# Linear attention: the transposes of a pair's keys ahead of the next pair's query features

## What is computed

```python
def _phi(x, proj):
    return jax.nn.elu(x @ proj) + 1.0
h = _ln(x, g1, beta1)
q = _phi((h @ wq).reshape(b, s, H, DH), proj)
k = _phi((h @ wk).reshape(b, s, H, DH), proj)
v = (h @ wv).reshape(b, s, H, DH)
# per token t, with running sums over the tokens up to it:
kv = kv + k_t[..., :, None] * v_t[..., None, :]
ksum = ksum + k_t
out = einsum('bhd,bhde->bhe', q_t, kv) / (einsum('bhd,bhd->bh', q_t, ksum) + 1e-06)
```

## Time and profile before

| | us |
|---|---|
| median of three runs | 2431.95 |
| the profiled execution | 2432.54 |
| its span, first to last instruction | 2430.7 |
| linear attention in the timeline | about 1287 to 1862 |

### The profile page before, as it was taken

The page is one execution under the profiler, slowest core; times in us unless marked ns, Lnnn a source line. Parts: engine busy times, 40 slices in busy tenths (PEclk is TensorE's granted clock), DMA queues, the critical chain, the costliest instruction groups (busy, mean ns, idle before and its releaser), DMA issues. The chain is left out here.

```text
span 2430.7 us, 40493 instructions
## 1 busy us (share of the span) xinstructions
PE 1889.6 (78%) x13801; PEld 1054.3 (43%) x13801; DVE 1596.5 (66%) x3655; ACT 913.7 (38%) x1452; POOL 501.3 (21%) x421
## 2 busy tenths in 40 slices
PE   1678788896279888999866999999997856678566
PEld 0244444443112222322234666666665634446344
DVE  1666666655288887788455666666665489855997
ACT  0033333354105554555644444444443321223122
POOL 1111111102322222220031000000001366600665
PEclk9788888897658998999979999999999978779787
DMA  6333323300232223333000000000000000000000
GB/s 159 57 55 54 52 53 54 54 16 0 36 51 50 50 49 45 43 53 53 2 0 1 2 1 2 2 2 3 2 1 1 1 0 0 1 1 0 5 13 18
DMA packets 71743, 63.26 MB, mean 26 GB/s; under 512 B 11528, under 2 KB 69384, under 8 KB 71560
## 3 DMA queue, kind: packets, MB, share of 16 engines
q1 hardware_dynamic: 71560, 60.87, 14.4%
HBM read 45.51 MB, written 15.20 MB: 25 GB/s over the span
## 5 line engine op out<-in xcount | busy, mean ns | idle before, releaser
L488 DVE TENSOR_REDUCE ab_M<-ps 128x1 f32<-128x512 f32 x512 | 331.0, 687 | 88.5 <-PE ps L372 77.2
L332 ACT ACTIVATE ab_probs<-ps 128x1024 f32<-128x1024 f32 x256 | 260.0, 1023 | 248.5 <-PE ps L399 248.1
L488 DVE TENSOR_REDUCE aa_M<-ps 128x1 f32<-128x384 f32 (+3 forms) x352 | 216.6, 640 | 158.9 <-PE ps L377 146.2
L332 ACT ACTIVATE aa_probs<-ps 128x1024 f32<-128x1024 f32 (+1 forms) x192 | 168.2, 881 | 287.5 <-PE ps L402 285.4
L372 PE MATMUL ps<-ab_KS,ab_QS 72*128 72x512 bf16 x512 | 217.0, 429 | 72.5 <-DVE ab_M L488 35.5
L372 PE MATMUL ps<-aa_KS,aa_QS 72*128 72x384 bf16 (+3 forms) x512 | 156.9, 342 | 119.5 <-DMA aa_KS<-aa_parts_dram 96.7
L1455 PE MATMUL ps<-gate_up,fp_xT 128*128 128x352 f32 x256 | 128.6, 668 | 92.5 <-DVE fp_xh L1497 91.1
L372 PEld LDWEIGHTS ps<-ab_KS,ab_QS 72*128 72x128 bf16 x512 | 51.1, 100 | 261.1 <-DVE ab_M L488 201.1
L416 PE MATMUL ps<-ab_probs,ab_V 128*9 128x512 f32 x1024 | 144.1, 636 | 21.4 <-ACT ab_probs L332 15.9
L399 PE MATMUL ps<-ab_QS,ab_KS 74*128 74x512 bf16 x512 | 159.5, 398 | 0.5 <-ACT ab_probs L332 0.5
L372 PEld LDWEIGHTS ps<-aa_KS,aa_QS 72*128 72x128 bf16 x512 | 54.9, 108 | 190.5 <-DMA aa_KS<-aa_parts_dram 63.2
(11 more groups left out here) (286 smaller groups left out, 3950.9 us busy)
## 6 DMA issues: line engine op xcount, KB each, us to landing
aa_QS<-aa_parts_dram SPq DMA_DIRECT2D x144, 64.0 KB
aa_KS<-aa_parts_dram SPq DMA_DIRECT2D x144, 64.0 KB
ab_QS<-ab_parts_dram SPq DMA_DIRECT2D x144, 64.0 KB
ab_KS<-ab_parts_dram SPq DMA_DIRECT2D x144, 64.0 KB
aa_parts_dram<-aa_splitq SPq DMA_DIRECT2D x24, 128.0 KB, 1.8
aa_parts_dram<-aa_splitk SPq DMA_DIRECT2D x24, 128.0 KB, 1.9
ab_parts_dram<-ab_splitq SPq DMA_DIRECT2D x24, 128.0 KB, 1.8
ab_parts_dram<-ab_splitk SPq DMA_DIRECT2D x24, 128.0 KB, 1.9
```

The lines of the kernel that those rows point to most:

```text
L332: act.activation(v(probs[r][:]), v(src), ACT.Exp, scale=scale).then_inc(scores_free, 1)
L488: v.tensor_reduce(M[:, heads[0]:heads[-1] + 1, qt], src, AX.X, ALU.max).then_inc(max_free, 1)
```

## The change

One line of the list. For each pair j, before:

```diff
-        STEP += [(new[0], "phiq", new[1]), (MAIN, "ktok", j), (new[0], "phik", new[1]),
+        STEP += [(MAIN, "ktok", j), (new[0], "phiq", new[1]), (new[0], "phik", new[1]),
                  (older[0], "attnT", older[1])]
```

## The result

The changed kernel takes 2448.57 us (median of 14 runs, 2440.0 to 2459.17) against 2428.33 us (14 runs) for the kernel before: ratio 1.0093, 95% interval 1.0073 to 1.0112. The forecast was 1.1% slower, 2458 us with a range of 2445 to 2468, from a base of 2431.95; the difference of the medians is +20.2 us against +25.9 forecast. The interval of the ratio, on a base of 2428.33, is +18 to +27 us.

What follows compares the result with a forecast made beforehand. The prediction took ScalarE's and VectorE's chains behind the phiq matmuls as the pace setters. Its terms, 25.3 - 1.6 + 2.2 = +25.9 us on a median of 2431.95, gave 2458 us, 1.1% slower, range 2445 to 2468.

Steps and rivals of the forecast that it cites:

- three terms: Parts of the forecast sum: 25.3 us for v pairs, -1.6 for other pairs, +2.2 for the layer's start.
- The view of the bound: Linear attention: ScalarE's and VectorE's chains, both started by the phiq matmuls, set the pace; TensorE's busy share hides this.
- v pairs: Pairs with a v matmul last: transposes then wait for la_V; +0.87 or +0.95 us each, 28 pairs, +25.3 us.
- everything behind (phik, masks, state copy, next v) hangs on ezk with no slack: In v pairs, the next v matmul moves by the same +0.87 us as the start of ezk.
- Other pairs: Pairs with no v matmul last: -0.05 us each, 32 pairs, -1.6 us.
- The wait moves; it doesn't go: Pairs without v last: TensorE waits about 0.65 us ahead of state instead of 0.5 ahead of the attn transposes.
- Start: First three pairs of the layer: phiq follows the waiting key transposes; +2.2 us at the hT transposes, bounds 1 and 3.5.
- The covered uses: hT stands ahead of y, and y covers the copy of v 7; the pair behind costs nothing.
- A: Rival: TensorE alone sets the layer's pace, other chains have slack; -6.9 us, 2425 us; chance 0.07.
- B: Rival: the removed wait counts in full and the V copy's wait is covered; -31 us, 2401 us; chance 0.03.
- C, the clock: Rival: the clock falls in the 28 v pairs; +31 us on top, 2489 us; chance 0.06.
- The rule on micro-idles: Frequent micro-idles between matmul groups can switch the clock's level; weighed for this layer, where 1.00 was expected to stay.

Runs made afterwards that it cites:

- e4: Kernel before, with only ScalarE's Ktok copy moved ahead of the queries' exponential (ez); linear attention layer -15.1 us.
- e7: The changed kernel, with ScalarE's attnT copy moved ahead of the keys' exponential (ez); layer +14.0 us against the change.
- e5: Kernel before, with only ScalarE's Ktok copy moved later, between below and ez of the keys; layer +37.5 us.
- e3: The changed kernel, with the last v of pairs 3 to 6 moved between the next pair's phiq and phik; layer 536.25 us, 14.6 less than before.
- e2: Kernel before, with the key transposes first in pairs 0 to 3 alone; layer -0.2 us.
- e1: Kernel before, with the key transposes first in pairs 4 to 7 alone; layer +20.5 us.
- e6: The changed kernel, with phiq first again in pairs 0 to 2 of the first item's pass; layer 566.34 us, 2.6 less than with the change.
- e8: Kernel before, with the Ktok copy between below and ez of the queries (pairs 0-3), transposes first and last v between phiq and phik (4-7); ratio 0.9885.

## Why the prediction was right, step by step

**The number.** The measured 2448.57 us is 9.4 us below the forecast and in the range. Of these, 3.6 us are the base: 14 runs of the kernel before have a median of 2428.33, where the forecast started from 2431.95 with three. The rest is the change, +20.2 us instead of +25.9. Two of the three terms came out a little below their own bounds: +20.7 against 21 to 28, and -4.4 against -3.2 to +3.2. The lowest sum of the bounds, 2431.95 + 21 - 3.2 + 1 = 2450.75, is above the measured time; it is the allowance for the scatter of the runs that covers it. The mechanism is what was right, more than the sizes.

**The view of the bound** held in the main. The share of busy time says TensorE (94% in an item); the pace is set by ScalarE's and VectorE's chains behind phiq, with one link that the prediction didn't see: before, the masks on VectorE waited for TensorE's scores (next paragraph). e4 and e7 show it: TensorE's biggest wait taken away gives 0.12 to 0.18 us of 0.49 to 0.54, and 33 us of waits at L1006 taken away, at the price of later key features, give a slower kernel.

**v pairs: +25.3 forecast, +20.7 measured.** The mechanism and the number of waits (28) were right, the size was 0.75 us a pair, not 0.87 or 0.95. The terms of the wait were right: 1.78 - 0.92 = 0.86 at the transposes, +0.38 for the transposes ahead of phiq (1788.18 to 1788.56), and ezk 1.78 behind belowq (1789.62 to 1791.40), as 2.15 - 0.37. The step that failed is "everything behind (phik, masks, state copy, next v) hangs on ezk with no slack". Before, the masks hung on the scores, not on the key features. The scores and the first mask of the pair of the earlier trace rows, and the key features and masks of an early item, in the kernel before:

```profile
1562.12 1.16 PE L995 MATMUL ps<-la_phiq,la_phik 64*128 64x128 f32 x16
...
1563.39 0.69 DVE L1087 TENSOR_TENSOR la_S<-ps,keep_kq 128x512 f32<-128x512 f32 x1
```
```profile
1513.09 0.69 DVE L1078 SCALAR_TENSOR_TENSOR la_phik<-ps,la_ezk 128x512 f32<-128x512 f32 x1 [0.83 <-ACT la_ezk L936]
...
1513.88 1.29 DVE L1087 TENSOR_TENSOR la_S<-ps,keep_kq 128x512 f32<-128x512 f32 x2
```

They start 0.73 us (1562.66 to 1563.39) and 0.79 us behind the key features; after, and in e4, it is 0.61 and 0.60. It is so in nearly all pairs: from 1330 to 1840 us the distance is 0.73 in 26 pairs and 0.79 in 25 before, 0.60 or 0.61 in all after and in e4, and mostly 1.36 to 1.42 in e5, where the wait for Ktok is 0.5 us longer. The masks need the scores as well, and before, the scores (1562.12 + 1.16 = 1563.28, just ahead of the mask at 1563.39) were late because the attn transposes ahead of them had waited for Ktok. With that wait gone, VectorE runs on without the 0.12 and 0.18 us. 0.87 - 0.12 = 0.75; 0.95 - 0.18 = 0.77; both forms of v pair measure +0.75. That is the whole value of the removed wait in these pairs, and the sum had it at nothing. The idle column shows no gap there, only the distance from start to start does.

**Other pairs: -1.6 forecast, -4.4 measured**, -0.14 us a pair instead of -0.05. The same term, 0.12 to 0.18 us a pair, is missing from the sum. "The wait moves; it doesn't go" was right: 0.59 us at L1006 (0.65 forecast) for 0.49 to 0.54 at L1032.

**Start: +2.2 forecast, +3.05 measured at the same place** (+3.4 at the state matmuls of pair 3). The order costs 2.3 us (e3 at full clock), as carried through the first pairs; the other 0.7 go with the lower clock in that stretch (0.85). Whether the longer waits bring it on isn't settled. Of the four kernels with the change's start, three (after, e2, e7) have a stretch of 10 us with 0.83 to 0.85 within 20 us behind the first key transposes, and e3 has none; the six with the order of before at the start have none there. But e1 and e7 also have lower clocks in the set-up ahead of the first key transposes, where all the kernels are alike.

**The loop: 0 forecast, -1.7 measured.** The interval with the jump back of the hardware loop took 12.35 us before and 10.69 after. In each kernel it holds an idle time of TensorE, 2.2 to 3.2 us long, for which the profile shows no releaser, and behind it the clock differs (the kernel before, then after; columns as above):

```profile
1655.00:1665.00 10.00, 7.81 (x85) 5.58 (x86) 3.59 (x7) 3.32 (x6) 0.00 (x0) 0.83 0.02 4
```
```profile
1662.80:1672.80 10.00, 7.29 (x96) 5.79 (x96) 3.96 (x10) 3.32 (x6) 0.00 (x0) 1.00 0.02 6
```

The ten profiles fall into two groups by it: where the granted clock of the 10 us there is 1.00 (after, e2, e6, e7, e8), the interval takes 10.7 to 11.2 us; where it is 0.83 (before, e1, e3, e4), 12.2 to 12.6; and at 0.55 (e5), 15.9. So the -1.7 us go with the clock in two single executions. Why it falls in some and not in others isn't shown: the idle times overlap (2.4 to 3.2 us where it fell, 2.2 to 2.7 where it didn't). The order may have a part in it: of the five kernels with the transposes first in pair 0 the clock fell in one (e3), of the five with phiq first there in four (all but e8). Without this interval the layer is +19.7 us.

**The covered uses** (hT, and y ahead of pair 0) held: other than the 28, L984 shows one wait of 0.2 us for la_state, and one of 2.2 us at the loop's jump that has no releaser.

**Rivals.** A and B fell with e1, e2 and e4. **C, the clock:** over 1400 to 1640 us the granted clock is 1.00 after as before, with TensorE busy for 213.8 of 240 us instead of 224.8:

```profile
1400.00:1640.00 240.00, 213.81 (x2521) 156.14 (x2519) 147.96 (x384) 108.83 (x193) 6.04 (x6) 1.00 0.01 2
```

So two idle spells of 0.6 to 0.7 us in every v pair of 10.1 us didn't bring the clock down in this stretch. The rule on micro-idles of the Trainium skill ("TensorE: Matmul & The Clock Gate", section "A second HAM failure mode: psum-queue depth-cycling"), by which the clock can switch between its two levels, didn't show here.

## What to carry to other kernels

When several steps share one buffer and each hands it back through another engine's copy, look at the order as a string of uses and pieces of other work: two uses side by side cost the copy, and a piece of work taken from between them is a new wait even if it removes one elsewhere. Before crediting a removed wait, follow what the waiting engine does next up to the first thing that another engine releases; here that was 0.1 us away. And where ScalarE has two dependent steps in a row, an independent one between them cost less here than one behind them.

## What the runs showed of the hardware

ScalarE starts an instruction that doesn't need the one ahead about 0.1 us before that one's end as the profile shows it (Ktok at 1538.03 against belowq's end at 1538.14, ezq at 1538.40 against the copy's end at 1538.51), and a dependent one, which in this kernel waits for a semaphore that the one ahead raises, 0.03 us after it (before: belowq 1559.85 + 0.60 = 1560.45, ezq 1560.48). Whether the reading of the data or the semaphore holds it back, no run here tells apart. Put between the two, the 0.47 us copy costs 0.23 us of the chain instead of 0.37. Over some 60 pairs of the layer that is about 8 us, an estimate from 0.14 us a pair.
